# A transformer layer with latent attention and 18 experts: LayerNorm groups issued one group apart, and attention slots two apart

## The reference

```python
def layernorm(x): return (x - mean(x)) / sqrt(var(x) + 1e-5)

def attention(x):
    k_eff = (Wq.T @ Wuk).reshape(nh, hs, nl)
    v_eff = transpose((Wuv.T @ Wo.T).reshape(nl, nh, hs), (1, 0, 2))
    c_kv  = x @ Wdkv.T                                    # [B, T, 512]
    q     = (x @ Wq.T) split into heads
    q_lat = einsum('bhts,hsl->bhtl', q, k_eff)
    attn  = softmax(causal(einsum('bhtl,bkl->bhtk', q_lat, c_kv) / sqrt(hs)))
    y_lat = einsum('bhtk,bkl->bhtl', attn, c_kv)
    return einsum('bhtl,hld->bhtd', y_lat, v_eff) heads side by side

x = x + attention(layernorm(x))
x = x + ffn(layernorm(x))        # h + shared experts + top-2 of 16, h = layernorm(x)
```

## Time and profile before

| | us |
|---|---|
| median of 2 runs | 8930.98 (8891.42 to 8970.53) |
| the profiled execution | 8360.59 |
| its span (slowest core, 6) | 8359.5 |
| spans of the 8 cores | 8318.7 to 8359.5 |
| mean granted TensorE clock, share of full speed | 0.84 on every core |

### The profile page before, as it was taken

How to read it: one execution, slowest core, us unless ns; L and a number is a source line. 1 busy time by engine, 2 the same in 40 slices (tenths; PEclk the granted TensorE clock), 3 DMA queues, 4 the chain that set the end, 5 groups by cost and what they waited for, 6 DMA issues and landing times. The chain is left out here.

```text
span 8359.5 us, 70779 instructions; the slowest of 8 cores (8318.7 to 8359.5 us)
## 1 busy us (share of the span) xinstructions
PE 5596.0 (67%) x26400; PEld 2533.0 (30%) x26400; DVE 2315.2 (28%) x4075; ACT 1608.9 (19%) x2949; POOL 607.1 (7%) x495
## 2 busy tenths in 40 slices
PE   2354454556566656656654488888888888888888
PEld 1132222222222222222221233333333333333333
DVE  0000111033333333343332322222222222222222
ACT  1111211212222222222222111111111111111111
POOL 0011212100000000000002200010000000000000
PEclk8677777777887887888786799999999999999998
DMA  5311111100000000000000444444444444444443
GB/s 184 127 31 61 31 40 40 31 10 6 3 3 3 3 6 3 3 3 3 6 0 3 121 131 122 129 121 121 121 121 121 121 121 121 121 130 133 131 134 101
DMA packets 721526, 589.12 MB, mean 70 GB/s; under 512 B 26258, under 2 KB 667538, under 8 KB 714642
## 3 DMA queue, kind: packets, MB, share of 16 engines
q1 hardware_dynamic: 721188, 584.58, 24.3%
HBM read 567.74 MB, written 16.78 MB: 70 GB/s over the span
## 5 line engine op out<-in xcount | busy, mean ns | idle before, releaser
L819 PE MATMUL pball<-arena 128*128 128x512 bf16 x2304 | 896.6, 389 | 513.1 <-DVE arena L763 426.9
L878 PE MATMUL pball<-arena 128*128 128x512 bf16 x2304 | 888.0, 385 | 32.2 <-POOL arena L852 28.8
L821 PE MATMUL pball<-arena 128*128 128x512 bf16 x2304 | 895.3, 389 | 0.0
L524 PE MATMUL pball<-arena 128*128 128x512 bf16 x2304 | 741.1, 494 | 221.9 <-DVE arena L514 221.9
L880 PE MATMUL pball<-arena 128*128 128x512 bf16 x2304 | 887.5, 385 | 0.0
L834 PE MATMUL pball<-arena 128*128 128x512 bf16 x2304 | 873.2, 379 | 0.0
L836 PE MATMUL pball<-arena 128*128 128x512 bf16 x2304 | 873.2, 379 | 0.0
L758 ACT ACTIVATE arena<-arena 128x1024 bf16<-128x1024 f32 x432 | 454.4, 1056 | 2090.1 <-PE pball L880 969.2
L468 PE MATMUL pball<-arena 128*128 128x512 bf16 x2304 | 591.8, 399 | 284.1 <-ACT arena L479 172.0
L763 DVE CAST arena<-arena 128x1024 bf16<-128x1024 f32 x432 | 479.4, 1131 | 707.5 <-DMA arena<-rw 520.7
L509 PE MATMUL pball<-arena 128*128 128x128 bf16 x2304 | 249.0, 268 | 536.1 <-DVE arena L514 536.1
(11 more groups left out here) (127 smaller groups left out, 4380.2 us busy)
## 6 DMA issues: line engine op xcount, KB each, us to landing
arena<-rw SPq DMA_DIRECT2D x512, 512.0 KB, 5.2
arena<-rg SPq DMA_DIRECT2D x256, 512.0 KB, 5.3
arena<-xall SPq DMA_DIRECT2D x16, 2048.0 KB, 10.4
arena<-sw SPq DMA_DIRECT2D x64, 512.0 KB, 5.3
arena<-wq SPq DMA_DIRECT2D x8, 2048.0 KB, 11.2
arena<-wot SPq DMA_DIRECT2D x8, 2048.0 KB, 10.4
arena<-wqt SPq DMA_DIRECT2D x8, 2048.0 KB, 10.2
arena<-sg SPq DMA_DIRECT2D x32, 512.0 KB, 5.2
```

The source lines that it names most:

```text
L524: ins = pe.matmul(bankf(pvb), ptb[:, j, :], ckv_tm[:, j, :], start=(j == 0), stop=(j == 4 * c - 1))
L819: pe.matmul(bankf(0), rgb_[wpar][:, ic, :], ln2[:, ic, 0:512], start=(ic == 0), stop=(ic == 15))
L821: i1 = pe.matmul(bankf(1), rgb_[wpar][:, ic, :], ln2[:, ic, 512:1024], start=(ic == 0), stop=(ic == 15))
L878: pe.matmul(bankf(bb0), rw2b[:, fc, dc * 128:(dc + 1) * 128], hsl[:, fc, 0:512], start=(fc == 0), stop=(fc == 7))
```

## The change

Stages 1a and 1b: `ln_group` is split into `ln_S` (statistics up to the spread rows) and `ln_T` (multiply and subtraction). The loop issues load g, `ln_S` of g, and then normalisation and projection of g-1; the last group's follow the loop. `lng` and the spread rows are doubled; the temporary stays single. The load semaphore is split by parity. The waits of the projection on ScalarE's newest count become waits for the last eviction of the same bank (`cons_free`). The copy to `x1` moves into the second part.

Attention: a third `pbuf` and third sets of the small statistics; the loop keeps up to three slots open, so the order is A0, A1, A2, B0, A3, B1, A4, B2 and so on, and B125, B126, B127 at the end. `load_head` is called at slot 2 instead of 1. The PV bank follows the slot number as before.

```diff
+    ln_rows_free = [0]
+    ln_apply_po = [0, 0]
+    ln_apply_ve = [0, 0]
+    ln_tmp_free = [0]
+    ln_bcast = [0, 0]
+
+    def ln_S(x_f32, ntok, rstd_sb, mrs_sb, par):
+        wge(pe, SXp[par])
+        wge(ac, SXp[par])
         wge(pe, SAC)
...
         wge(ac, SPE)
+        wge(ac, SDV, ln_rows_free[0])
         SAC.inc(ac.activation(mean, PS[0:1, 0, 0:ntok], AF.Copy, scale=1.0 / D), 1)
...
         SDV.inc(ve.tensor_mul(mean2, mean, rstd), 1)
+        ln_rows_free[0] = SDV.n
...
         wge(ac, SPE)
+        wge(ac, SPO, ln_apply_po[par])
+        wge(ac, SDV, ln_apply_ve[par])
         SAC.inc(ac.activation(rstd_sb[:, 0:ntok], PS[:, 6, 0:ntok], AF.Copy), 1)
         SAC.inc(ac.activation(mrs_sb[:, 0:ntok], PS[:, 7, 0:ntok], AF.Copy), 1)
-        wge(po, SAC)
+        ln_bcast[par] = SAC.n
+
+    def ln_T(x_f32, ln_out, ntok, rstd_sb, mrs_sb, tmp_big, par, lng_free_val):
+        wge(po, SAC, ln_bcast[par])
+        wge(po, SDV, ln_tmp_free[0])
         for c in range(16):
             ins = po.tensor_mul(tmp_big[:, c, 0:ntok], x_f32[:, c, :], rstd_sb[:, 0:ntok])
         SPO.inc(ins, 1)
+        ln_apply_po[par] = SPO.n
         wge(ve, SPO)
-        wge(ve, SPE)
+        wge(ve, SPE, lng_free_val)
         for c in range(16):
             ins = ve.tensor_sub(ln_out[:, c, :], tmp_big[:, c, 0:ntok], mrs_sb[:, 0:ntok])
         SDV.inc(ins, 1)
+        ln_apply_ve[par] = SDV.n
+        ln_tmp_free[0] = SDV.n
...
+    def stage1a_T(g):
         par = g % 2
...
+        wge(po, SXp[g % 2], sx_done[g])
         SPO.inc(po.tensor_copy(x1[:, :, g * 256:(g + 1) * 256], xst[par]), 1)
+        ln_T(xst[par], lng[par], 256, rstd1a[par], mrs1a[par], tmp1a, par,
+             lng_free[par])
+        wge(pe, SDV, ln_apply_ve[par])
         for jc in range(16):
             b = 2 + jc % 2
-            wge(pe, SAC)
+            wge(pe, SAC, cons_free[b])
...
             SAC.inc(ac.activation(qbuf[:, jc, :], bankf(b, 0, 256), AF.Copy), 1)
+            cons_free[b] = SAC.n
+        lng_free[par] = SPE.n
         wge(sy, SAC)
         SQO.inc(sy.dma_start(out=qscr[:, g * 256:(g + 1) * 256].rearrange('(c p) t -> p c t', p=128),
                              in_=qbuf), 16)
+
+    for g in range(4):
+        wge(sy, SPO)
+        SXp[g % 2].inc(sy.dma_start(out=xst[g % 2],
+                            in_=xown[:, g * 256:(g + 1) * 256].rearrange('(c p) t -> p c t', p=128)), 16)
+        sx_done[g] = SXp[g % 2].n
+        ln_S(xst[g % 2], 256, rstd1a[g % 2], mrs1a[g % 2], g % 2)
+        if g >= 1:
+            stage1a_T(g - 1)
+    stage1a_T(3)
...
+    for g in range(16):
+        wge(sy, SPO)
+        SXp[g % 2].inc(sy.dma_start(out=xstb[g % 2],
+                            in_=xall[:, g * 256:(g + 1) * 256].rearrange('(c p) t -> p c t', p=128)), 16)
+        ln_S(xstb[g % 2], 256, rstd1b[g % 2], mrs1b[g % 2], g % 2)
+        if g >= 1:
+            stage1b_T(g - 1)
+    stage1b_T(15)
...
-        par = it % 2
+        par = it % 3
         if si == 0:
             wge(pe, SQIp[hp], 48 * (h // 2 + 1))
-        if si == 1 and h + 1 < NH:
+        if si == 2 and h + 1 < NH:
             load_head(h + 1)
...
-        pvb = 4 + par
+        pvb = 4 + st['it'] % 2
...
+    slots = [(h, si) for h in range(NH) for si in range(NSLOT)]
+    pend2 = []
+    for it, (h, si) in enumerate(slots):
+        if len(pend2) >= 3:
+            stb = pend2.pop(0)
+            attn_b(stb)
+            if stb['si'] == NSLOT - 1:
+                attn_epi(stb['h'])
+        pend2.append(attn_a(it, h, si))
+    for stb in pend2:
+        attn_b(stb)
+        if stb['si'] == NSLOT - 1:
+            attn_epi(stb['h'])
```

More of the change, by code:

```diff
@@ L37 @@
 MAP['xst'] = A0 + 65536
-MAP['xbf'] = A0 + 98304
-MAP['lng'] = A0 + 106496
+MAP['lng'] = A0 + 98304
 MAP['qbuf'] = A0 + 114688
@@ L44 @@
 MAP['xst_b'] = A0 + 16384
-MAP['xbf_b'] = A0 + 49152
-MAP['lng_b'] = A0 + 57344
+MAP['lng_b'] = A0 + 49152
 MAP['tmp1b'] = A0 + 65536
@@ L59 @@
 MAP['ylatt_all'] = A0 + 52224
+MAP['pbuf3'] = A0 + 60416
 MAP['rw2'] = 12032
@@ L148, in inc @@
             return instr
-    SW = Sem('sw'); SX = Sem('sx'); SQO = Sem('sqo')
+    SW = Sem('sw'); SQO = Sem('sqo')
+    SXp = [Sem('sx0'), Sem('sx1')]
     SWp = [Sem('sw0'), Sem('sw1')]
@@ L175, in ac_edge @@
         wge(ac, SAC)
-    for s in (SW, SX, SWp[0], SWp[1], SWs[0], SWs[1], SWs[2],
+    for s in (SW, SXp[0], SXp[1], SWp[0], SWp[1], SWs[0], SWs[1], SWs[2],
               SQIp[0], SQIp[1], SQO, SSM, SOUT, SPE, SAC, SDV, SPO):
@@ L225, in build_program @@
     lnsq_gate = [0, 0]
-    def ln_group(x_f32, ln_out, ntok, rstd_sb, mrs_sb, tmp_big):
-        wge(pe, SX)
-        wge(ac, SX)
+    ln_rows_free = [0]
[6 more added lines that the diff above has]
+        wge(ac, SXp[par])
         wge(pe, SAC)
@@ L328, in build_program @@
            for i in (0, 1)]
-    lng = carve('lng', [128, 16, 256], BF16)
+    lng = [carve_at(MAP['lng'] + i * 8192, 8192, BF16).rearrange('p (a b) -> p a b', a=16)
+           for i in (0, 1)]
     qbuf = carve('qbuf', [128, 16, 256], BF16)
     tmp1a = carve('tmp1a', [128, 16, 256], F32)
-    rstd1a = carve_at(MAP['rstd1a'], 1024, F32)
-    mrs1a = carve_at(MAP['rstd1a'] + 1024, 1024, F32)
-    for g in range(4):
-        par = g % 2
[L337 to L341, removed]
+    rstd1a = [carve_at(MAP['rstd1a'] + i * 2048, 1024, F32) for i in (0, 1)]
+    mrs1a = [carve_at(MAP['rstd1a'] + i * 2048 + 1024, 1024, F32) for i in (0, 1)]
+    cons_free = {2: 0, 3: 0, 4: 0, 5: 0}
+    lng_free = [0, 0]
+    sx_done = {}
+    def stage1a_T(g):
+        par = g % 2
+        wge(po, SXp[g % 2], sx_done[g])
         SPO.inc(po.tensor_copy(x1[:, :, g * 256:(g + 1) * 256], xst[par]), 1)
-        ln_group(xst[par], lng, 256, rstd1a, mrs1a, tmp1a)
-        wge(pe, SDV)
+        ln_T(xst[par], lng[par], 256, rstd1a[par], mrs1a[par], tmp1a, par,
+             lng_free[par])
+        wge(pe, SDV, ln_apply_ve[par])
         for jc in range(16):
             b = 2 + jc % 2
-            wge(pe, SAC)
+            wge(pe, SAC, cons_free[b])
             for ic in range(16):
                 ins = pe.matmul(bankf(b, 0, 256), wqt_sb[:, ic, jc * 128:(jc + 1) * 128],
-                                lng[:, ic, :], start=(ic == 0), stop=(ic == 15))
+                                lng[par][:, ic, :], start=(ic == 0), stop=(ic == 15))
             SPE.inc(ins, 1)
@@ L367, in build_program, with stage1b_T @@
             for i in (0, 1)]
-    lngb = carve('lng_b', [128, 16, 256], BF16)
+    lngb = [carve_at(MAP['lng_b'] + i * 8192, 8192, BF16).rearrange('p (a b) -> p a b', a=16)
+            for i in (0, 1)]
     tmp1b = carve('tmp1b', [128, 16, 256], F32)
-    rstd1b = carve_at(MAP['rstd1b'], 1024, F32)
-    mrs1b = carve_at(MAP['rstd1b'] + 1024, 1024, F32)
+    rstd1b = [carve_at(MAP['rstd1b'] + i * 2048, 1024, F32) for i in (0, 1)]
+    mrs1b = [carve_at(MAP['rstd1b'] + i * 2048 + 1024, 1024, F32) for i in (0, 1)]
     ckv_tm = carve('ckv_tm', [128, 32, 512], BF16)
     ckv_fm = carve('ckv_fm', [128, 4, 4096], BF16)
-    for g in range(16):
+    def stage1b_T(g):
         par = g % 2
[L377 to L382, removed]
+        ln_T(xstb[par], lngb[par], 256, rstd1b[par], mrs1b[par], tmp1b, par,
+             lng_free[par])
+        wge(pe, SDV, ln_apply_ve[par])
         for kt in range(2):
             b = 2 + kt
-            wge(pe, SAC)
+            wge(pe, SAC, cons_free[b])
             for ic in range(16):
-                ins = pe.matmul(bankf(b), lngb[:, ic, kt * 128:(kt + 1) * 128],
+                ins = pe.matmul(bankf(b), lngb[par][:, ic, kt * 128:(kt + 1) * 128],
                                 wdkvt_sb[:, ic, :], start=(ic == 0), stop=(ic == 15))
@@ L391, in build_program @@
             SAC.inc(ac.activation(ckv_tm[:, g * 2 + kt, :], bankf(b), AF.Copy), 1)
+            cons_free[b] = SAC.n
         for lc in range(4):
             b = 4 + lc % 2
-            wge(pe, SAC)
+            wge(pe, SAC, cons_free[b])
             for ic in range(16):
                 ins = pe.matmul(bankf(b, 0, 256), wdkvt_sb[:, ic, lc * 128:(lc + 1) * 128],
-                                lngb[:, ic, :], start=(ic == 0), stop=(ic == 15))
+                                lngb[par][:, ic, :], start=(ic == 0), stop=(ic == 15))
             SPE.inc(ins, 1)
@@ L400, in build_program @@
             SAC.inc(ac.activation(ckv_fm[:, lc, g * 256:(g + 1) * 256], bankf(b, 0, 256), AF.Copy), 1)
+            cons_free[b] = SAC.n
+        lng_free[par] = SPE.n
+    for g in range(16):
[6 more added lines that the diff above has]
+    stage1b_T(15)
     nc.all_engine_barrier()
-    pbuf = [carve_at(MAP['pbuf'] + i * 8192, 8192, BF16) for i in (0, 1)]
+    pbuf = [carve_at(MAP['pbuf'] + i * 8192, 8192, BF16) for i in (0, 1)] + \
+           [carve_at(MAP['pbuf3'], 8192, BF16)]
     ptb = carve('pt', [128, 32, 128], BF16)
@@ L413, in build_program @@
     masks = carve('masks', [128, 8, 512], BF16)
[L414 to L420, removed]
```

(13 more changed lines are left out.)

## The result

| | before | after |
|---|---|---|
| ratio after / before | | 0.9443 (95%: 0.9243 to 0.9644) |
| median of all runs | 8875.95 (10 runs) | 8484.42 (13 runs) |
| profiled execution | 8360.59 | 7919.68 |
| spans of the 8 cores | 8318.7 to 8359.5 | 7886.4 to 7918.6 |

The kernel is faster by 5.6%, by this ratio. The ratio rests on two executions of each kernel, 8350.69 and 8432.94 before, 7919.68 and 7929.57 after. The second of before lies high: seven more executions of that kernel, timed beside the experiments, took 8352.27 to 8367.55. Against those, and between the two profiled executions, the gain is 5.2 to 5.3%, or 441 us between the profiled ones.

What follows compares the result with a forecast made beforehand. TensorE was taken to idle behind a serial chain in 1a and 1b, and behind VectorE's copies in attention. Gains of 295 (1b), 118 (1a) and 0 (attention) sum to 413 us, from 8930.98 to 8518; range 8390 to 8660.

Steps and rivals of the forecast that it cites:

- the two load gaps: Stage 1a: groups 2 and 3 still wait 14.1 us each before their statistics, the load queued behind the q write.
- the stall at T(3): Stage 1a, last group: its first eviction waits until the previous group's q is written; 4 us of stall taken.
- The unknown, matmuls past a reader: Stages 1a and 1b: how cleanly matmuls run past a PSUM reader; 122 us less gain if that brings nothing.
- The first rival: Attention gains too: TensorE's wait is for the same slot's softmax, so distance removes 669 us; time about 7850; chance 0.06.
- my bound of 20: Attention: bounds of -20 to +30 us set around an expected change of 0.
- my own sign of a shorter stretch: Attention: a stretch shorter than 2710 to 2760 us was named as proving the prediction wrong.
- the 0 that I took for attention: Attention: waits before the transposes stay, since the copies stand behind an equally long VectorE tail; gain 0.
- The slower rival: Attention: the new pairing holds TensorE at 1.2 GHz, +458 to +708 us against -413, time 8976 to 9226; chance 0.04.
- the exposed load: Stage 1b rival: the load, felt from 44 us after issue, eats the whole gain at 63; time 8813; chance 0.01.
- I take the same 413 from it: Sum: the 413 us gain of stages 1a and 1b taken off the shown median 8930.98, giving 8518 us.
- first line, 8360.6 to 7948: Sum: the 413 us gain taken off the profiled execution, 8360.6 to 7948 us.

Runs made afterwards that it cites:

- the first experiment: LayerNorm half alone: the changed kernel with attention as in the kernel before; spans of 7897.5 to 7923.0 us on cores 0 to 3.

## Why the prediction was right and where it was wrong

- **Stage 1b: right.** Gain 295 predicted, 293 measured; period 39.5 against 40.0 in the mean; stage 645 against 650.6. T(g-1) waits for the subtraction behind S(g)'s row operations, as argued, 3.33 us where the working gave 3.6. Putting the subtraction first removes this wait and 50 us, which shows it. What makes the period longer is T: its 32 matmuls of 512 columns, 8.45 in the working, take 9.3 us on average in the steady groups.
- **Stage 1a: right.** 118 against 118. T was 30.7 us where I took 29.5; the two load gaps were 13.1 and 12.6 where I took 14.1, and the stall at T(3) 2.71 where I took 4. That the errors cancel to the microsecond is luck.
- **The unknown, matmuls past a reader: right.** 122 us predicted; 119 by putting the waits back, 105 by taking them away in the old order. No clock gain came on top: taking the waits away in the old order made the 512-column matmuls slower in the mean. The overlap of groups, the other part, is shown by the difference only.
- **Attention: right in what bounds it, wrong by a little in size.** The wait is VectorE's order, not the softmax of the same slot. The distance alone brought 10 to 17 us, with 5 to 7 us off the waits, and the order alone took 563 us away. The first rival is refuted: a large removable wait exists (I priced it at 669 us; the new order took 438), but distance does not reach it. The stretch came out at 2753.6, inside the 2710 to 2760 that I named, but that is luck: the range goes round the 2732 of the earlier trace rows, a window that ended 46 us before the stage did. Against the true 2775.1 the gain is 21, just past my bound of 20, and by my own sign of a shorter stretch the 0 that I took for attention was too low. Most of what moved is how fast the matmuls ran: PV was 741 us busy before and 705 after, the scores 592 and 609. The rule of the Trainium skill that I weighed (Perfetto Trace Analysis, "Per-engine timelines": strictly first in, first out on VectorE) was borne out by the trace of every kernel with this order, and by the 563 us when the order changed.
- **The slower rival and the exposed load did not come.** The granted clock of the attention stretch was 0.80 against 0.81, and 1b's loads show no wait after the first.
- **Wrong: the base of the sum.** The step "I take the same 413 from it" put the gain on the median of the two runs shown, 8930.98, and left 570 us above the profiled execution unexplained. Both of those runs were prolonged. Its own first line, 8360.6 to 7948, was the better forecast: the two executions that count took 7920 and 7930, 18 to 28 less. The range of 8390 to 8660 was built round the other base, and so excludes them. The median of all 13 runs, 8484.42, lies in it, but that is no hit: it depends on how many of the 13 were prolonged and by how much, for which the working has no term. The range is also narrower than its own working, whose bounds were 8470 to 8670 with 40 more on either side. Of the 28 us left between 7948 and 7919.7, attention makes 21 and the stretch after it 4, both taken as 0. The traces of later runs show where such an excess can sit: in one execution of the first experiment above, the stretch after attention took 3856.8 us on core 0 and 4083.6 on core 4 with the same instructions. I had the spans of the profiled execution and a gap of 6.8% between it and the median in front of me, and should have let the range hold both bases.

## What to carry to other kernels

Before adding a buffer or a slot of distance, find what stands ahead of the late instruction in its own engine's order: here TensorE waited 751 us for copies, a third buffer left that alone, and moving one block of VectorE work behind the copies removed 438 of them. A wait for the newest count of a semaphore is a wait for everything issued so far; naming the last reader of the same bank was worth 105 to 119 us by itself. When the profiled execution and the median of a few runs lie far apart, state the gain against the profiled one and let the range hold both.

## What the runs showed of the hardware that was not expected

- The clock took part in the attention runs. Removing 438 us of waits in attention also took 164 us off the matmuls, which were the same ones, as the granted clock of the stretch went from 0.80 to 0.92. Distance alone made PV some 34 us shorter and the scores some 19 longer in the old order, and the matmuls together 38 longer in the new one. None of this is in the waits.
- Identical attention code took 2763.8, 2773.6 and 2775.1 us in three kernels that differ in the stages before it. Most cores of one execution agree to 0.2 us, so this is not noise of single cores, but it is one traced execution of each kernel. The scores were 584 us busy in the first and 590 to 593 in the other two, which is part of it. The cause was not tried.
- The same 32 projection matmuls took between 8.3 and 10.0 us from one group to the next, in the same loop, each time behind the same wait of 3.33 us. The granted clock was 0.50 in the first 1.2 us of each of these 15 pieces and 1.00 from 7 us on. A difference of 1.5 us between two kernels in one such group therefore says nothing; the mean of all groups does.
